# Keys of an attention block kept once, with the right end of the relative table carried by extra query and key rows

## What is computed

```
qkv = q @ in_proj_weight.T + in_proj_bias        # split in q, k, v; 16 heads of 16
qh = qh / math.sqrt(d)
scores = jnp.einsum('bhid,bhjd->bhij', qh, kh)
rel = jnp.clip(pos[None, :] - pos[:, None], -K, K) + K          # K = 64
bias_r = jnp.einsum('bhid,rd->bhir', qh, rel_pe)                # 129 values a query
bias = take_along_axis(bias_r, rel)                             # one for each key
attn = jax.nn.softmax(scores + bias, axis=-1)
out = (attn @ vh) -> [b, l, e] @ out_w.T + out_b
x = layernorm(x + out);  x = layernorm(x + ffn(x))              # ffn: 256 -> 1024 -> 256, gelu
```

## Time and profile before

| | us |
|---|---|
| median of 3 runs | 2366.7 |
| lowest and highest of them | 2362.38 and 2367.46 |
| the profiled execution, its own time | 2361.56 |
| span of its trace | 2359.6 |
| TensorE matmuls busy | 2227.5 (94%) |
| VectorE busy | 1739.1 (74%) |
| ScalarE busy | 1573.1 (67%) |
| GpSimd busy | 1085.8 (46%) |

### The profile page before, as it was taken

One profiled execution on the slowest core, in us unless ns is written; L12 is line 12 of the kernel. 1 busy time (PEld: TensorE's weight loads), 2 busy tenths in 40 slices (PEclk: granted clock), 3 DMA queues, 4 the chain that ended last, 5 costly groups with the idle time before them and its releaser, 6 DMA issues. The chain is left out here.

```text
span 2359.6 us, 47824 instructions
## 1 busy us (share of the span) xinstructions
PE 2227.5 (94%) x14580; PEld 1261.9 (53%) x14580; DVE 1739.1 (74%) x3447; ACT 1573.1 (67%) x2192; POOL 1085.8 (46%) x1803
## 2 busy tenths in 40 slices
PE   8996899999999999999999999999999998899997
PEld 5563444444444444444444444444444443688886
DVE  4443777777777777777777777777777772788885
ACT  3433377777777777777777777777777776466766
POOL 1001444554445544455445545454554431567663
PEclk9998599999999999999999999999999999899999
DMA  9997777777777777777777677777777752333421
GB/s 305 400 352 265 204 208 202 210 214 211 206 207 208 208 213 209 210 203 208 212 209 212 201 208 215 209 208 202 210 213 209 209 178 73 100 102 111 111 65 45
DMA packets 334570, 468.55 MB, mean 199 GB/s; under 512 B 89797, under 2 KB 262550, under 8 KB 334486
## 3 DMA queue, kind: packets, MB, share of 16 engines
q0 software_dynamic: 120960, 215.78, 33.9%
q1 hardware_dynamic: 204358, 243.32, 32.7%
q10 hardware_dynamic: 9168, 8.52, 1.1%
HBM read 244.73 MB, written 221.25 MB: 197 GB/s over the span
## 5 line engine op out<-in xcount | busy, mean ns | idle before, releaser
L933 ACT ACTIVATE probs<-weigh_ps 128x1024 f32<-128x1024 f32 x1024 | 1048.9, 1025 | 471.8 <-PE weigh_ps L1100 468.0
L985 DVE CUSTOM_DVE_ANT_1 ring_ps<-ring_ps,band_all 128x512 f32<-128x512 f32 x1008 | 681.0, 716 | 263.8 <-PE ring_ps L1061 263.6
L1061 PE MATMUL ring_ps<-keys,queries 48*128 48x512 f32 x2048 | 827.1, 468 | 40.1 <-DVE partial_max L974 14.0
L1100 PE MATMUL weigh_ps<-queries,keys 50*128 50x512 f32 (+3 forms) x2688 | 751.0, 385 | 1.3 <-ACT probs L933 0.6
L974 DVE TENSOR_REDUCE partial_max<-ring_ps 128x2 f32<-128x1024 f32 x512 | 627.7, 1226 | 112.3 <-PE ring_ps L1061 80.8
L1061 PEld LDWEIGHTS ring_ps<-keys,queries 48*128 48x128 f32 x2048 | 370.7, 187 | 524.7 <-issue 398.9
L1117 PE MATMUL sum_ps<-probs,values 128*32 128x512 f32 x4096 | 546.6, 605 | 0.1
L839 POOL COPY carried<-carried 128x252 f32<-128x252 f32 x430 | 159.3, 396 | 568.2 <-ACT carried L922 568.2
L1085 PE MATMUL weigh_ps<-ident,band_all 128*128 128x128 f32 x2048 | 363.2, 290 | 19.3 <-ACT carried L922 16.5
L1100 PEld LDWEIGHTS weigh_ps<-queries,keys 50*128 50x128 f32 x2688 | 356.3, 186 | 14.9 <-ACT probs L933 9.5
L1085 PEld LDWEIGHTS weigh_ps<-ident,band_all 128*128 128x128 f32 x2048 | 213.6, 141 | 249.9 <-ACT probs L933 104.6
(11 more groups left out here) (119 smaller groups left out, 1857.3 us busy)
## 6 DMA issues: line engine op xcount, KB each, us to landing
band_scr<-carried SPq DMA_DIRECT2D x256, 512.0 KB, 4.8
band_all<-band_scr POOLq DMA_DIRECT2D x128, 512.0 KB, 5.4
band_all<-band_scr POOLq DMA_DIRECT2D x128, 256.0 KB, 4.4
keys<-k_scr POOLq DMA_DIRECT2D x128, 240.0 KB, 8.1
k_scr<-k_parts SPq DMA_DIRECT2D x16, 1792.0 KB, 9.8
q_scr<-q_parts SPq DMA_DIRECT2D x16, 1024.0 KB, 10.4
queries<-q_scr POOLq DMA_DIRECT2D x128, 128.0 KB, 3.8
o_scr<-weighted_s SPq DMA_DIRECT2D x64, 256.0 KB, 7.6
```

What stands on the lines that cost most here:

```text
L933: nc.scalar.activation(probs[:, u % PROBS], weigh_ps[weigh_of["scores", at]][:], ACT.Exp).then_inc(s_pr, 1)
L985: nc.vector.tensor_tensor_reduce(out=both, in0=both, in1=bias, scale=1.0, scalar=LOWEST, op0=ALU.add, op1=ALU.max, accum_out=partial_max[: ...
L1061: nc.tensor.matmul(dst, query_rows(c, h, ROWS, tile * P, (tile + 1) * P), key_rows(c, h, ROWS, c0, c0 + 512), start=True, stop=True, tile_ ...
L1100: last = nc.tensor.matmul(weigh_ps[weigh_of["scores", at]][:, h, e0 * P:e1 * P], key_rows(c, h, QROWS, k0, k0 + P), query_rows(c, h, QROWS ...
```

## The change

The keys are stored once, with the left end of the table; KCOLS falls from 15 tiles to 9 (tile 0 stands once more behind tile 7). The right end is added by six pairs of rows (ENDS = 6, PARTS = 2, so 12 rows a head): on the side of the queries row e holds q·(right end − left end) for the queries of tile e and zero elsewhere, on the side of the keys row e is 1 for key tiles from e+2 on and 0 before. A product of 60 rows (LOOK_ROWS) then holds the right bias for every pair of tiles, and 62 rows (QROWS) the minus maximum too.

In stage one this takes a new product of 32 columns wide weights (`wdT`), four f32 matmuls of 512 columns for each sequence, an evacuation by ScalarE and one by VectorE, four small stores to the new `d_scr`, a zeroing of `d_scr` before (6.3 MB), and some set-up of the weights. The evacuations with `bk_right` go. In stage two the queries get two more loads a step, `weigh` is no longer split, and the far looks and the near looks take other key tiles. The set-up of stage two gets three POOL instructions for `beyond` and two DMAs.

```diff
-    QROWS = ROWS + 2
+    ENDS = NT - 2
+    LOOK_ROWS = ROWS + ENDS * PARTS
+    QROWS = LOOK_ROWS + PARTS
-    RIGHT = NT - 2
-    KCOLS = (RIGHT + NT + 1) * P
+    KCOLS = (NT + 1) * P
...
+        def load_ends(eng, i, c):
+            for h in range(HG):
+                r0 = h * ROW_TILE + ROWS
+                eng.dma_start(queries[r0:r0 + ENDS * PARTS, c % SLOTS].bitcast(F32),
+                              d_scr[(i * SLOTS + c) * HG + h]).then_inc(s_d[c % SLOTS], 16)
...
                 if half == 0:
-                    return [(0, HALF, RIGHT * P, bk_right), (HALF, 512, RIGHT * P, bk_left), (2 * P, 512, -2 * P, bk_right)]
-                return [(0, 512, RIGHT * P + 512, bk_left), (0, 512, 512 - 2 * P, bk_right)]
+                    return [(0, HALF, 0, bk_right), (HALF, 512, 0, bk_left)]
+                return [(0, 512, 512, bk_left)]
...
+                sp.dma_start(d_scr, over(zeros[:].rearrange("p n c -> p (n c)"), ENDS * PARTS, 1)).then_inc(s_zd, 16)
                 sp.dma_start(w1_s, w1.rearrange("(j p) e -> p j e", p=P)).then_inc(s_w, 16)
...
+                        sp.wait_ge(s_dlo, b + 2)
+                        sp.sem_inc(s_passed, 1)
+                        sp.wait_ge(s_zd, 16)
+                        for half in range(2):
+                            tiles = min(QUARTERS, ENDS - half * QUARTERS)
+                            for part in range(PARTS):
+                                own = d_scr[bass.ds(b * H, H), half * QUARTERS * PARTS + part, half * 512:half * 512 + P]
+                                sp.dma_start(flat_tiles(own, tiles),
+                                             d_parts[half * PAD:half * PAD + H, a, part, 0:tiles * P].bitcast(F32)
+                                             .rearrange("h (t c) -> h t c", c=P)).then_inc(s_store[a], 16)
...
+                        act.wait_ge(s_djob, b + 1)
+                        nc.scalar.activation(d_parts[:, a, 0], bank[0][0:2 * PAD, :], ACT.Identity,
+                                             bias=bd_col[:, 0:1]).then_inc(s_dhi, 1)
...
+                for h in range(HG):
+                    r0 = h * ROW_TILE + PAD
+                    nc.vector.memset(queries[r0:r0 + PAD].bitcast(F32), 0.0).then_inc(s_zq, 1)
...
+                pe.wait_ge(s_block, 5)
+                for kt in range(KE):
+                    for j in range(2):
+                        nc.tensor.matmul(bank[5][:, kt * PAD:(kt + 1) * PAD], w_in_s[:, j, kt * P:(kt + 1) * P],
+                                         ends_block[:, j, 0], start=(j == 0), stop=(j == 1))
+                pe.wait_ge(s_bias, 16)
+                for j in range(2):
+                    last = nc.tensor.matmul(bank[6][0:2 * PAD, 0:1], ends_block[:, j].rearrange("p a h -> p (a h)"),
+                                            b_col[:, j:j + 1], start=(j == 0), stop=(j == 1))
...
+                                pe.wait_ge(s_vev, b * 4 + 5)
+                                for half in range(2):
+                                    c0 = HALF + half * 512
+                                    for kt in range(KE):
+                                        last = nc.tensor.matmul(bank[0][half * PAD:(half + 1) * PAD, :], wdT[:, kt],
+                                                                xT[:, a, kt, c0:c0 + 512], start=(kt == 0),
+                                                                stop=(kt == KE - 1), tile_position=(0, half * PAD))
+                                last.then_inc(s_djob, 1)
...
+                sp.wait_ge(s_beyond, 3)
+                for h in range(HG):
+                    row = keys[h * ROW_TILE + ROWS:h * ROW_TILE + LOOK_ROWS].bitcast(F32)
...
+                nc.gpsimd.memset(beyond[:], 1.0).then_inc(s_beyond, 1)
+                pool.wait_ge(s_beyond, 1)
+                nc.gpsimd.affine_select(out=beyond[:], in_=beyond[:], compare_op=ALU.is_ge, fill=0.0, base=-3,
+                                        pattern=[[2, NT + 1], [0, P]], channel_multiplier=-1).then_inc(s_beyond, 1)
+                pool.wait_ge(s_beyond, 2)
+                nc.gpsimd.memset(beyond[:, NT], 0.0).then_inc(s_beyond, 1)
...
-                    rights = sum(1 for t in tiles if n > t + 1)
-                    for e0, e1 in ((0, rights), (rights, QT)):
-                        if e0 < e1:
-                            k0 = key_tile(n, g * QT + e0) * P
-                            last = nc.tensor.matmul(weigh_ps[weigh_of["scores", at]][:, h, e0 * P:e1 * P],
...
+                    last = nc.tensor.matmul(weigh_ps[weigh_of["scores", at]][:, h],
+                                            key_rows(c, h, QROWS, n * P, (n + 1) * P),
+                                            query_rows(c, h, QROWS, g * 512, (g + 1) * 512),
```

More of the change, by code:

```diff
@@ L485, in _ @@
                 pe.wait_ge(s_evd, 2)
+                pe.wait_ge(s_wdc, 1)
                 with pe.Fori(0, B // 2) as i:
@@ L698, in cnt, with look_tile @@
                 return i * (SLOTS * per_step) + value
-            def key_tile(n, tile):
-                return RIGHT + n if n <= tile + 1 else n - 2
+            def look_tile(tile, half):
+                near = tile // QT * QT + tile % 2
+                return near if half == 1 else (near + QT) % NT
             block = ctx.enter_context(nc.Block())
@@ L762, in _ @@
                 for h in range(HG):
-                    row = keys[h * ROW_TILE + ROWS:h * ROW_TILE + QROWS].bitcast(F32)
+                    row = keys[h * ROW_TILE + LOOK_ROWS:h * ROW_TILE + QROWS].bitcast(F32)
                     sp.dma_start(flat(row, 0, [row.ap[0], [P, SLOTS * KCOLS // P], [1, P]]),
@@ L852, in step_of @@
                         load_queries(pool, i, step + 3)
+                        load_ends(pool, i, step + 3)
                     read_chunk(i, step, 0)
@@ L1156, in _ @@
                     if step == 0:
-                        pe.wait_ge(s_one, 16 * HG)
                         pe.wait_ge(s_set, 6)
                     for m in range(NT):
+                        if step == -2 and m == QT:
+                            pe.wait_ge(s_one, 16 * HG * 2)
                         pair(0, step, m)
```

107 lines of the change are left out of this document (79 added, 28 removed).

## The result

The changed kernel takes 2376.7 us (median of 5 runs, 2373.7 to 2380.3), the kernel before 2364.4 (2360.4 to 2367.5): a ratio of 1.0054, 95% interval 1.0037 to 1.0071. It is slower, as forecast, but by 12 us and not by 25. The profiled execution took 2373.7 us with a span of 2371.9; that of before had a span of 2359.6, so the two traces also stand 12.3 us apart and can be laid side by side.

What follows compares the result with a forecast made beforehand. Both stages were taken to be bound by TensorE, with stage one's DMAs just keeping up. 24 + 2.5 + 4.5 − 6 = +25 us gave 2386.6 on the profiled execution, 2391.7 on the median's scale; forecast 2390, range 2376 to 2404.

Steps and rivals of the forecast that it cites:

- Rival 2: Stage one: DMA sets the pace, fewer stores shorten it and hide the new product; 2340, 0.08 together with rival 3.
- Part 1: Stage one: the new product adds 3.0 us a sequence on TensorE, started in order; +24 us (15 to 27).
- My lower bound: New product of stage one: both halves side by side, four records deep, 1.9 us.
- Part 2: Stage one: the evacuations with the right end and 12 MB of key stores leave; 0 us.
- Part 3: Set-up of stage one: end weights delay the first sequence, +2.5 us (1 to 4); clearing query rows 0 us (0 to 2).
- Part 4: Stage one: 6.3 MB of zeros in SP's queue delay the first stores by 16 us but hide; 0 us (0 to 6).
- Rival 4: Stage one: zeros at half rate hold the stores, ScalarE and TensorE wait; +35 to +40, 2403, chance 0.12.
- Part 5: Set-up of stage two: SP waits for `beyond` before its first band store, delaying VectorE's first look; +4.5 us (3 to 6).
- Part 6: Stage two: unsplit weighs save 0.1 us a step over 64 steps; −6 us (0 to −9).
- Rival 3: Stage two: removed weight loads lay on TensorE's path, gain of 30 us; 2366, 0.08 together with rival 2.
- Part 7: Stage two: two more loads a step on POOL, 1.0 us, go into its waits; 0 us.
- Rival 1: Stage one: halves of the new product run side by side, 15 us in place of 24; 2382, chance 0.25.

Runs made afterwards that it cites:

- e2: Changed kernel with the new product's four matmuls on 8 columns in place of 512, most end differences left out; 2365.4 us, ratio 1.0012 to the kernel before.
- e3: Changed kernel with the new product on three column groups of 256 columns in place of two of 512; 2369.1 us, ratio 1.0037 to the kernel before.
- e11: Changed kernel with both halves of the new product on the first column group, half the end differences not computed; 2389.4 us, ratio 1.0125.
- e1: Changed kernel with the weighs of five units a step split in two again; 2449.7 us, ratio 1.0372 to the kernel before.
- e5: Changed kernel with ones and step rows of the keys in one table built in stage one, one transfer for each head; 2371.8 us, ratio 1.0047.
- e9: Changed kernel with three of the five pairs of products split again; 2381.7 us, ratio 1.0083 to the kernel before.
- e6: Changed kernel with the new product on three column groups, put behind the next sequence's transposes in TensorE's gap; 2366.9 us, ratio 1.0026.
- e7: e6 combined with e5, and the output weights' transposes ahead of the end weights; 2358.1 us, ratio 0.9992 to the kernel before.
- e12: e7 with the keys' constant rows sent behind the first band store (first slot) and the fifth (other three); 2358.3 us, ratio 0.9994.
- e8: Kernel before with 40 copies of a two-column product at its start, so stage two's loop stands 160 instructions further back; 2443.1 us, ratio 1.0350.
- e4: Changed kernel with the three POOL steps that build beyond moved into stage one; 2375.8 us, ratio 1.0054 to the kernel before.

## Why the prediction was right or wrong

**Direction and bound: right.** That stage one is TensorE's, that a product added to it is added to the time, and that fewer evacuations and fewer bytes give nothing back, is what the 32 waits, the 23.94 and 25.98 us and e2, e3 and e11 show. Rival 2 is out for this kernel. That much of the mechanism was right; the forecast of +25 is twice the measured 12 by the size of one term, and that size hung on how the column groups work.

**Part 1, the new product, is the step that failed.** It was taken at 3.0 us, 8 x 3.0 = 24; it is 1.85 us, with 0.1 us on either side where it meets its neighbours, 2.04 a sequence and 16.3 in all. The failing choice was "an engine that starts its matmuls in order". The records start in pairs every 0.43 us, and since records on one group never do that (e11), the second of a pair is on the other column group, ahead of records that stand earlier in the program. My lower bound, read off the weighted sum, was right to 0.05 us; the row nearest in kind (several column groups, same shape) should have had the vote over an argument from the order of issue. The strict order of start and end in the Trainium skill's "TensorE: Matmul & The Clock Gate", Part 3, which I let weigh in, is not what this trace shows. The Trainium skill's "TensorEngine Tiling (Array Packing)", under Key Properties, says of tiles that they operate independently, and with that the trace agrees (1.85 us for eight records). My upper bound, all eight one after the other, was 3.4 us; e11 has 3.55.

**Part 2** right: nothing came back. **Part 3** right, 2.6 for 2.5, but by one trace each: in e1 to e5, e9 and e11, with the same start of TensorE, the first key product starts 1.3 to 3.1 us later than in the kernel before. The clearing of the query rows takes 3.47 us each, for at most 4.9, and stalls nobody.

**Part 4, the zeros,** right for this kernel: the first stores leave 16.0 us later, as worked out, and hide. But the margin was worth a sentence that is missing: it is gone as soon as TensorE gets 1.6 us a sequence faster (e2), and in e6 and e7 the stall costs 7.7 and 9 us once. Rival 4 had the mechanism, for a kernel that was not this one.

**Part 5** right, +4.5, by the chain that was named: 3.3 us of it until the store's issue, 1.1 from there to the look. That the whole of it and 4 us more can be won back (e12, 16.2 us for 20.2 before) was not foreseen.

**Part 6, the unsplit products,** -6 and measured -6.6; e9 gives 0.055 us a step for three of the five. Two more gains were in no term: -2.5 us behind the last exponential and -1.7 us in step 0. The end scatters over all traces here, from 361.7 to 366.6 us, and in e8, which has the old code there, it is 361.7; so the -2.5 is most likely scatter. Step 0 is another matter: 31.19 us in both traces of the old code (before and e8), 29.4 to 30.7 in the others, so that part of the -1.7 may be the change's. What in it does this stays open. Rival 3 is out: e9, with three fifths of the removed matmuls back, has a step of 26.89.

**Part 7** right: POOL is busy 479.6 of 900 us for 447.7, and the steps show nothing of it.

What the forecast missed altogether is a side of the change that costs nothing now but could have decided it. e1's loop has the length of that of the kernel before, 1714 instructions; it only stands 60 further back, behind what the change adds to stage one and to the first steps. Had the change kept the split products, its new code ahead of the loop would have cost another 66 us (the 73 of e1 less 7 for the splits). What saves it is part 6, not by the 0.1 us a step, but because the loop is 80 instructions shorter and so ends at 2701.

On the sum: 16.3 + 2.6 + 4.5 - 6.6 = 16.8, less the 1.7 and 2.5 just told, is 12.6 (12.3 measured). Rival 1's 2382 was within 6 us, and the truth lies at the lower end of the range because these two small gains, which nobody forecast, came on top of it: that 2376.7 is still inside the range is in part luck.

## What to carry to other kernels

When a matmul is added on part of the columns, price it by the deepest column group, not by the number of matmuls, and give the halves groups of their own; then look for a wait of TensorE's into which it fits, because in a stage that TensorE bounds that is the whole of its price. Then look what the faster stage runs into: in e6 and e7 one wait for a store took 7.7 and 9 us back. Count the instructions of a long loop on each engine before and after an edit: a loop that grows, or only moves, over one block of the program more can cost more than any matmul in it. When an experiment shifts code by adding instructions, subtract what these cost themselves (16.6 of the 82 us of e8) before reading the rest. And when a stall seems to be one count shared by several stores, count them apart, but expect the next store to be waiting behind it.

## What the runs showed of the hardware

TensorE's loop of 1714 instructions cost nothing at one place of the program and 4.9 us a turn 160 instructions further back (e8: 69 us in 14 turns): nine packets of 16 KB a turn were loaded where there had been none, TensorE waited 3.4 us at each return, and behind that its clock was at half for about 4 us. Eight f32 records of 512 columns took 1.85 us on two column groups and 3.55 us on one (e11), started in pairs against their order in the program. VectorE cleared 4096 columns of f32 on 32 partitions in 3.47 us, 0.85 ns a column, less than the 1.2 ns of its pass over 1024. A store of 0.5 MB could be read 8.35 us after its issue in the kernel before, 8.7 and 7.8 us with 0.4 to 0.5 MB right ahead of it in its queue (the changed kernel, e4), and 12.1 to 12.3 us with 0.5 MB ahead of it at the very start of the stage (e7, e5).
